# Graph attention with layer norm on one core: gathering rows of x itself instead of rows of a node table

## What is computed

```python
messages = x[col]                               # col = dst
gate = messages @ W_gate.T + b_gate             # one number an edge
h = messages @ W_lin.T + b_lin
seg_max = segment_max(gate, row)                # row = src
e = exp(gate - seg_max[row]); denom = segment_sum(e, row) + 1e-16
pooled = segment_sum(e / denom[row] * h, row)
x = layernorm(x + pooled @ W_out.T + b_out)
```

## Time and profile before

| | us |
|---|---|
| three runs: median (lowest to highest) | 2847.6 (2842.83 to 2848.6) |
| span of the profiled execution, first to last instruction | 2844.9 |
| DVE busy | 1676.2 |
| POOL busy | 1748.5 |
| PE busy | 1008.8 |
| ACT busy | 174.1 |

### The profile page before, as it was taken

One profiled execution on the slowest core, in us unless ns is written; L12 is line 12 of the kernel. 1 busy time (PEld: TensorE's weight loads), 2 busy tenths in 40 slices (PEclk: granted clock), 3 DMA queues, 4 the chain that ended last, 5 costly groups with the idle time before them and its releaser, 6 DMA issues.

```text
span 2844.9 us, 25631 instructions
## 1 busy us (share of the span) xinstructions
PE 1008.8 (35%) x5080; PEld 835.6 (29%) x5080; DVE 1676.2 (59%) x5604; ACT 174.1 (6%) x664; POOL 1748.5 (61%) x1792
## 2 busy tenths in 40 slices
PE   3012112225233342433334243342433424333377
PEld 3011111224232232422323233232333323233255
DVE  9969998346455464645546455464655646455454
ACT  0421110000000000000000000000000000000025
POOL 0411002777777777777777777777777777777621
PEclk9999996565566665566656556565655656566566
DMA  3020001222222222222222222222222222223924
GB/s 115 3 92 0 0 0 29 54 54 54 55 53 55 53 55 54 54 55 53 55 53 54 54 54 54 54 53 55 53 55 54 55 53 54 54 54 67 41 50 122
DMA packets 91745, 148.65 MB, mean 52 GB/s; under 512 B 30393, under 2 KB 61970, under 8 KB 91588
## 3 DMA queue, kind: packets, MB, share of 16 engines
q0 software_dynamic: 56224, 117.06, 20.8%
q1 hardware_dynamic: 34767, 31.04, 3.5%
q10 hardware_dynamic: 722, 0.20, 0.0%
HBM read 134.35 MB, written 13.83 MB: 52 GB/s over the span
## 4 chain that ended last, share of the span: by engine, by line
POOL 43%; issue 23%; DVE 17%; PE 7%; DVEq 2%; another core or an unknown queue 2%; ACT 2%; DMA 2%; ACTq 1%; POOLq 0%
POOL arena L375 42%; DVE spread L916 3%; DVE nodes_sb L922 2%; PE bank L590 2%; PE bank L634 2%; DMA arena<-node_table,gather_at 1%; DVE rows_b L751 1%; DVE rows_a L750 1%; DVE rows_a L751 1%; POOL gate_prod L362 1%; DVE rows_b L750 1%; ACT gate_junk L430 1%; DVEq L952 1%; DVE turn_b L751 1%
## 5 line engine op out<-in xcount | busy, mean ns | idle before, releaser
L375 POOL DMA_INDIRECT arena<-node_table,gather_at x1757 | 1675.1, 953 | 790.6 <-issue 530.3
L590 PE MATMUL bank<-arena,spread 128*128 128x129 f32 x3520 | 736.9, 379 | 334.5 <-DVE nodes_sb L922 220.6
L590 PEld LDWEIGHTS bank<-arena,spread 128*128 128x128 f32 x3520 | 642.8, 276 | 424.5 <-DVE nodes_sb L922 291.4
L916 DVE TENSOR_SCALAR spread<-iota_row,place_t,weights 128x128 f32<-128x128 f32 x1760 | 599.0, 357 | 184.7 <-PE bank L590 83.0
L922 DVE SCALAR_TENSOR_TENSOR nodes_sb<-nodes_sb,weights,bank 128x129 f32 x1760 | 605.6, 344 | 55.2 <-PE bank L590 10.5
L894 DVE TENSOR_TENSOR_SCAN run_max<-pen,bank 40x128 f32<-40x128 f32 (+1 forms) x45 | 18.5, 411 | 756.8 <-PE bank L572 756.8
L572 PE MATMUL bank<-ident,arena 128*40 128x128 f32 (+1 forms) x45 | 17.3, 384 | 703.0 <-DMA arena<-node_table,gather_at 703.0
L572 PEld LDWEIGHTS bank<-ident,arena 128*40 128x40 f32 (+1 forms) x45 | 5.4, 119 | 711.0 <-issue 711.0
L552 PE MATMUL bank<-ident,dst_f 40*128 40x40 f32 x44 | 13.1, 297 | 235.7 <-DVEq L725 234.2
L542 PE MATMUL bank<-ident,rows_a 128*128 128x128 f32 x112 | 28.1, 429 | 180.0 <-DVE rows_a L776 144.7
L446 ACT ACTIVATE gather_at<-bank 128x40 int32<-128x40 f32 x44 | 8.9, 203 | 1258.6 <-PE bank L557 1229.2
(11 more groups left out here) (161 smaller groups left out, 1066.0 us busy)
## 6 DMA issues: line engine op xcount, KB each, us to landing
arena<-node_table,gather_at POOLq DMA_INDIRECT x1757, 20.6
node_table<-nodes_sb SPq DMA_DIRECT2D x1, 6347.7 KB
nodes_sb<-in_x SPq DMA_DIRECT2D x1, 6250.0 KB
rows_a<-in_x SPq DMA_DIRECT2D x13, 448.0 KB, 4.1
out<-rows_b SPq DMA_DIRECT2D x13, 448.0 KB, 3.3
k<-sorted_keys SPq DMA_DIRECT2D x132, 20.0 KB
turn_a<-in_src SPq DMA_DIRECT2D x1, 828.0 KB
turn_b<-in_dst SPq DMA_DIRECT2D x1, 828.0 KB
```

Source lines behind the costliest of these rows:

```text
L375: pool.indirect_dma_start(out=gathered_rows[par][:, t, :], out_offset=None, in_=table[:, :], in_offset=bass.IndirectOffsetOnAxis(ap=gather ...
L590: last = pe.matmul(tile_ps(slot), lhsT=spread[:, slot, :], rhs=gathered_rows[par][:, b * BATCH + u, 0:WIDTH], start=True, stop=True)
L916: return dve.tensor_scalar(spread[:, slot, :], iota_row[:, :], place_t[par][:, t:t + 1], weights[par][:, 0, t:t + 1], ALU.is_equal, ALU.mult)
```

## The change

The node table, its load, its ten products, its 101 activations and its store are gone. The gather reads rows of 512 bytes (128 floats) from `x`. The column of ones is set once, in both buffers, by POOL after the histogram (`hist_ready`). DVE computes gates when a chunk's rows are there: `find_gates` multiplies the rows by `wg`, which it has put into PSUM once (`wg_ps`), and sums 129 terms a row, the last of which is the bias that ACT has placed. DVE instead of PE now waits for the gathered rows; PE waits for `gates_found`. `sums` has memory of its own, and POOL zeroes it right at the start.

```diff
-        nodes_sb = sb("nodes_sb", [P, 13000])
+        sums = sb("sums", [P, BLOCKS * WIDTH]).ap()
+        gate_terms = arena[:, 14000:14000 + T * WIDTH].rearrange("p (t f) -> p t f", f=WIDTH)
+        gates = sb("gates", [P, T])
...
-            sp.dma_start(node_rows[:, :, 0:FEAT], x.rearrange("(p n) f -> p n f", n=NODE_COLS)).then_inc(x_loaded, 16)
-
-            sp.wait_ge(gates_ready, 1)
-            sp.wait_ge(ones_ready, 1)
-            sp.dma_start(table.rearrange("(p n) f -> p n f", n=NODE_COLS), node_rows).then_inc(table_stored, 16)
             sp.wait_ge(zero_ready, 1)
             sp.dma_start(skeys[0:1].rearrange("(a n) -> a n", a=1), zero_key[:, :]).then_inc(keys_stored, 16)
+            sp.wait_ge(iotas_ready, 1)
...
             pool.drain().then_inc(iotas_ready, 1)
 
-            pool.wait_ge(x_loaded, 16)
-            pool.wait_ge(weights_loaded, 16 * 6)
-            pool.memset(node_rows[:, :, FEAT:FEAT + 1], 1.0).then_inc(ones_ready, 1)
-            for c in range(NODE_COLS // GATE_COLS):
-                if c > 0:
-                    pool.wait_ge(prod_used, c)
-                pool.tensor_tensor(gate_prod[0:NODE_ROWS], node_rows[:, c * GATE_COLS:(c + 1) * GATE_COLS, 0:FEAT],
-                                   wg[0:NODE_ROWS].unsqueeze(1).to_broadcast([NODE_ROWS, GATE_COLS, FEAT]),
-                                   ALU.mult).then_inc(prod_ready, 1)
-
-            pool.wait_ge(table_stored, 16)
             pool.memset(sums, 0.0).then_inc(sums_blank, 1)
 
             pool.wait_ge(hist_ready, 1)
+            for par in range(2):
+                pool.memset(gathered_rows[par][:, :, FEAT:WIDTH], 1.0)
+            pool.drain().then_inc(ones_ready, 1)
...
-                    pool.indirect_dma_start(out=gathered_rows[par][:, t, :], out_offset=None, in_=table[:, :],
+                    pool.indirect_dma_start(out=gathered_rows[par][:, t, 0:FEAT], out_offset=None, in_=x[:, :],
...
             act.wait_ge(weights_loaded, 16 * 6)
-            for c in range(NODE_COLS // GATE_COLS):
-                act.wait_ge(prod_ready, c + 1)
-                for n in range(GATE_COLS):
...
-            act.activation(node_rows[:, :, FEAT + 1], gate_sum[0:NODE_ROWS, :], ACT.Identity,
-                           bias=bg[0:NODE_ROWS, 0:1]).then_inc(gates_ready, 1)
+            act.wait_ge(hist_ready, 1)
+            act.activation(gate_terms[:, :, FEAT], bg[:, 0:1].to_broadcast([P, T]), ACT.Copy).then_inc(bias_placed, 1)
...
             def turn_softmax(i, par, n=T):
 
+                pe.wait_ge(gates_found, i + 1)
                 pe.nop(nofuse=True)
-                pe.transpose(gate_rows[0:n], gathered_rows[par][:, 0:n, FEAT + 1], ident[:, :]).then_inc(gates_turned, 1)
+                pe.transpose(gate_rows[0:n], gates[:, 0:n], ident[:, :]).then_inc(gates_turned, 1)
...
-                    pe.wait_ge(rows_gathered[par], 16 * T * j + 16 * T)
                     turn_softmax(i, par)
...
+            dve.tensor_copy(wg_ps, wg[:, :])
...
+            def find_gates(par, at, n):
+                dve.tensor_tensor(gate_terms[:, at:at + n, 0:FEAT], gathered_rows[par][:, at:at + n, 0:FEAT],
+                                  wg_ps.unsqueeze(1).to_broadcast([P, n, FEAT]), ALU.mult)
+                dve.drain()
+                dve.tensor_reduce(gates[:, at:at + n], gate_terms[:, at:at + n, :], AX.X, ALU.add)
+                dve.drain().then_inc(gates_found, 1)
...
                     prepare(i + 1, j + par, 1 - par)
+                    dve.wait_ge(rows_gathered[par], 16 * T * j + 16 * T)
+                    find_gates(par, 0, T)
                     softmax(i, par)
                     add_tiles(i, i + 1, par, range(NB))
...
+            dve.wait_ge(rows_gathered[1], 16 * T * (CHUNKS // 2 - 1) + 16 * EARLY)
+            find_gates(1, 0, EARLY)
             softmax(CHUNKS - 1, 1, EARLY)
             add_tiles(CHUNKS - 1, CHUNKS, 1, range(EARLY // BATCH))
+            dve.wait_ge(late_gathered, 16 * (TILES - (CHUNKS - 1) * T - EARLY))
+            find_gates(1, EARLY, T - EARLY)
             softmax(CHUNKS, 1)
```

More of the change, by code:

```diff
@@ L79, in check_shapes @@
 def check_shapes():
-    assert P * MAIN_COLS + REST_ROWS * REST_COLS == EDGES and NODE_ROWS * NODE_COLS == NODES
+    assert P * MAIN_COLS + REST_ROWS * REST_COLS == EDGES
     assert EARLY % BATCH == 0 and CHUNKS % 4 == 0 and (CHUNKS - 1) * T + EARLY < TILES <= CHUNKS * T and (CHUNKS + 1) * T * P < KEYS + TAIL_ROWS * P
@@ L97, in sem @@
             return ctx.enter_context(nc.semaphore(name))
-        table = nc.dram_tensor("node_table", (NODES, ROW), F32).ap()
         skeys = nc.dram_tensor("sorted_keys", (1 + KEYS + TAIL_ROWS * P,), I32).ap()
@@ L114, in graph_attention @@
         part2_i = arena[:, 23 * EDGE_COLS // 2:23 * EDGE_COLS // 2 + EDGE_COLS].bitcast(I32)
[L115 to L118, removed]
+        gathered_rows = [arena[:, k * T * WIDTH:(k + 1) * T * WIDTH].rearrange("p (t f) -> p t f", f=WIDTH) for k in range(2)]
+        gate_terms = arena[:, 14000:14000 + T * WIDTH].rearrange("p (t f) -> p t f", f=WIDTH)
+        gates = sb("gates", [P, T])
         wg = sb("wg", [P, FEAT])
@@ L344, in _ @@
             sp.wait_ge(stored[1], 16 * (GROUPS // 2 + 1))
-            sp.wait_ge(table_stored, 16)
         @block.gpsimd
@@ L425, in _ @@
             act.wait_ge(weights_loaded, 16 * 6)
-            for c in range(NODE_COLS // GATE_COLS):
-                act.wait_ge(prod_ready, c + 1)
-                for n in range(GATE_COLS):
-                    at = c * GATE_COLS + n
-                    last = act.activation(gate_junk[0:NODE_ROWS], gate_prod[0:NODE_ROWS, n, :], ACT.Copy,
-                                          accum_out=gate_sum[0:NODE_ROWS, at:at + 1])
-                    act.drain()
-                act.drain().then_inc(prod_used, 1)
-            act.activation(node_rows[:, :, FEAT + 1], gate_sum[0:NODE_ROWS, :], ACT.Identity,
-                           bias=bg[0:NODE_ROWS, 0:1]).then_inc(gates_ready, 1)
+            act.wait_ge(hist_ready, 1)
+            act.activation(gate_terms[:, :, FEAT], bg[:, 0:1].to_broadcast([P, T]), ACT.Copy).then_inc(bias_placed, 1)
             for k, back, g, _ in turning:
@@ L886, in _ @@
             dve.wait_ge(sums_blank, 1)
+            dve.wait_ge(bias_placed, 1)
+            dve.wait_ge(weights_loaded, 16 * 6)
+            dve.tensor_copy(wg_ps, wg[:, :])
             dve.drain().then_inc(sums_added, 2 * BATCH)
+            def find_gates(par, at, n):
[4 more added lines that the diff above has]
+                dve.drain().then_inc(gates_found, 1)
             def softmax(i, par, n=T):
@@ L974, in _ @@
             prepare(CHUNKS - 1, CHUNKS // 2 - 1, 1)
+            dve.wait_ge(rows_gathered[0], 16 * T * (CHUNKS // 2))
+            find_gates(0, 0, T)
             softmax(CHUNKS - 2, 0)
             add_tiles(CHUNKS - 2, CHUNKS - 1, 0, range(NB))
+            dve.wait_ge(rows_gathered[1], 16 * T * (CHUNKS // 2 - 1) + 16 * EARLY)
+            find_gates(1, 0, EARLY)
             softmax(CHUNKS - 1, 1, EARLY)
             add_tiles(CHUNKS - 1, CHUNKS, 1, range(EARLY // BATCH))
+            dve.wait_ge(late_gathered, 16 * (TILES - (CHUNKS - 1) * T - EARLY))
+            find_gates(1, EARLY, T - EARLY)
             softmax(CHUNKS, 1)
```

19 lines of the change are left out of this document (6 added, 13 removed).

## The result

| | median us (lowest to highest) | ratio to the kernel before, 95% interval |
|---|---|---|
| kernel before | 2845.2 (2840.2 to 2848.6) | |
| changed kernel | 2820.8 (2820.4 to 2833.3) | 0.9921 [0.9899, 0.9944] |

The profiled execution has a span of 2819.4 us, 25.5 less than before, where the forecast had 15.0.

What follows compares the result with a forecast made beforehand. No engine bounds it throughout: DVE's serial sort, then POOL's gather issue, then an exposed end. Terms -17.1 - 25.7 + 7.1 + 0.5 + 0 + 20.2 = -15.0 on span 2844.9 gave 2829.9, so median 2832.6 us, range 2813 to 2855.

Steps and rivals of the forecast that it cites:

- The sort, -42.8: Sort before the gathers: removing the node table ends seven held DVE instructions (-17.1 us) and DVE's wait for ACT (-25.7 us).
- The memset, +7.1: Kernel start: the moved memset of sums holds DVE's cast until it ends, +7.1 us; bounds from 0 to held.
- Behind the histogram, +0.5: After the histogram: two small memsets and the iota may hold a small DVE operation, +0.5 us, at most 1.
- The loop, 0: Gather loop: 11.3 us of new DVE gate work a chunk hides in 13.8 us of slack, so 0 us.
- Rival A: Loop: gates outlast the slack, a chunk takes half the excess longer; about 2899 us; chance 9%.
- rival B: Loop: DVE's long operations keep POOL from issuing gathers; +198 us, 3031 us; chance 6%.
- the slack: Loop: 13.8 us between indices being ready and POOL needing them; 2.5 us left on average after the gates.
- The end, +20.2: Behind the last chunks gates are exposed: +11.3 for chunk 42, +5.3 early part, +3.6 late part.
- the forecast's own bounds for it: End: 13.8 us if the first delay, PE's late start on chunk 42, is covered too; 24.6 if there is no delay.
- C: Loop: unseen waits eat the cover, +13 us and 1 to 2 at the end; 2847 us, no change; chance 10%.
- D: Loop: the shorter row makes each gather 0.1 us cheaper, a chunk 46.8 us; about 2682 us; chance 5%.

Runs made afterwards that it cites:

- row 6400: Kernel before, all padding edges pointing to row 6400 in the middle of the table instead of row 0: 2844.7 us, ratio 0.9997.
- the sum twice: Changed kernel, each chunk's tensor_reduce in find_gates done twice: 2916.8 us, ratio 1.0249.
- spread rows: Padding edges read rows all over the table instead of row 0: 2819.1 us on the kernel before, 2808.4 us on the changed kernel.
- one sum in ten: Kernel before with all ten POOL products, but ACT sums only one node of ten: 2834.4 us, ratio 0.9963.
- ten tiles more: Changed kernel, ten tiles of each chunk summed once more in find_gates: 2827.5 us, ratio 0.9944.

## Why the prediction was right, point by point

- **The sort, -42.8**: right in sum, and the trace bears both parts out, -17.1 of held exchanges and -25.7 of waiting for ACT. But the parts are not separate prices. Shorter sums alone turned seven holds into ten, and moved the memset onto an operation that it holds. Without the products, 5.53 us of the 25.71 of waiting were left, so the products had made most of that wait too.
- **The memset, +7.1**: right, 6.9 in the trace, 6.8 in the run that moves it. No row of before decided between 0 and 7.1; the choice by the nearest row was a guess that came true.
- **Behind the histogram, +0.5**: nothing of it can be seen.
- **The loop, 0**: right. Product 5.49 and sum 5.53 us, as worked out from rows of other operations. Rival A's rule (half of the excess) and rival B's mechanism are real, and both were near: a second sum costs 96 us, the weights in SBUF 174. That a two-input operation holds a gather was read from the wrong row, as said above, and shown only by the run with the weights in SBUF. The step that was off is the slack, 13.8 us from the end of ACT's copies to POOL's next gather. POOL can start only 0.8 us after those copies end (1017.39, to 1018.21), and the shorter border of each pair decides. 11.3 us used up all but 1.2 to 1.5 of it, not all but 2.5.
- **The end, +20.2**: the term that was mis-sized; measured +8.4, plus 3.2 in the stretch before it, since the last chunk's first gather waited for its indices (53.38 us behind that of chunk 42, 50.23 before), 11.6 in all. That is below the forecast's own bounds for it, 13.8 to 24.6 (the second is 24.1 by its own terms, 11.3 + 5.3 + 7.5). The failed step is "some delay of PE on leaving its loop, which outlived the wait. I take it to come again behind the gates". There was no such delay: the rows came late, by reads of one row. The gates then lay in part under lateness that was there anyway. The scan of chunk 42 came 7.3 us later against the last gather, not 11.3, and the early scan another 1.0, not 5.3; beside it lies a stall of PE that took 10.6 us up to 2670 in the kernel before and 6.6 up to 2640 here. The late scan lost 3.5 (forecast 3.6) and stands 36.0 us behind the last gather, not 44. The stall, in the kernel before and then in the changed one:

```profile
2670.45 2.74 PE L590 MATMUL bank<-arena,spread 128*128 128x129 f32 x12 [10.62 <-issue]
```
```profile
2639.77 2.74 PE L565 MATMUL bank<-arena,spread 128*128 128x129 f32 x12 [6.56 <-issue]
```

  With the lateness removed from both kernels the end costs 25.5 us, near the forecast's own bound for no delay.
- **The output stage, not in the forecast**: 107.3 us from its first product on, 110.3 before. It goes with TensorE's granted clock in that stage, here for the kernel before, with row 6400, and with the sum twice (stretch, length, clock, DMA share, GB/s):

```profile
2734.65:2844.90 110.25, 0.69 0.39 108
```
```profile
2735.30:2848.60 113.30, 0.67 0.38 105
```
```profile
2813.70:2915.80 102.10, 0.78 0.43 117
```

  The levels are 0.5 (1.2 GHz) and 1.0 (2.4 GHz), and these are means between them. In all thirteen kernels the stage takes 110 to 113 us at 0.67 to 0.70, 105 to 107 at 0.72 to 0.76 (0.72 in the changed kernel, 0.73 and 0.72 with spread rows), and 102 at 0.78. So some 3 of the 25.5 us of span are no work of this change. They aren't the late reads of one row either: with one sum in ten, and with ten tiles more, these reads are there and the stage takes 105 us. Why the clock was what it was is not shown.
- **Rivals**: nothing in the runs speaks for C or D. POOL never waits between the chunks of the loop, and gathers of 512 and 520 bytes take the same 0.94 us.

So the forecast of the span was 10.5 us off (15.0, measured 25.5): 8.6 in the end (20.2, measured 11.6, of it 3 by the clock), 1.2 in the loop, where chunks are some 0.03 us shorter, and 0.7 at the start. The old kernel had a fault at its end that hid 14 us of the new work (25.5 - 11.6). Where that fault is mended first, the same change is worth 10.7 us instead of 24.

## What to carry to other kernels

A precomputed table that keeps other engines busy during a serial stage can cost more than many times its arithmetic done later, if that is done beside a stage set by something else (here 42.8 us against 485 us of new DVE work); but measure the cover there by the tightest of the waits that go round, and find the part behind the last overlap, where all of it shows. Place a long POOL memset beside DVE operations with two SBUF inputs, and a long DVE operation beside POOL with one input in PSUM. Let padding indices point to different rows: an idle time "for a DMA" that ends later than issue and usual landing explain should send one to the DMA share of that stretch before an engine is blamed.

## What the runs showed of the hardware

- **Many reads of one row are slow.** A gather of 128 times the same row moves 40 GB/s at a DMA share of 0.9, against 53 at 0.24 for different rows: 128 x 520 bytes at 40 GB/s are 1.66 us a gather, some 13 ns a read (an estimate from these rates), and more than POOL's 1.25 us between issues, so the queue runs late, by some 48 x 0.4 = 20 us at the end. In the changed kernel with 512 bytes it is 128 x 512 at 39 GB/s = 1.68 us. Whether it goes by reads or by bytes these runs can't tell: the rows differ by 1.6%, the rate of one kernel from stretch to stretch by more (37 to 44 GB/s).
- Beside it engines stand still at code that they run for the first time, waiting for nothing that the profile shows: PE for 10.6 us in the kernel before and 12.3 with row 6400, DVE for 4.99 in the changed one. With spread rows PE's is gone and DVE's is 2.40. But PE's stall is also missing, or no longer than 1.6 us, in two kernels that do read one row, those with the weights in SBUF and with ten tiles more. What makes these stalls is not shown.
- **A POOL memset holds a single-input DVE operation to its end** (9.17 us for 0.18; 8.49 for 0.76) and leaves two-input ones alone (0.55, 0.69). The Trainium skill has it so, by ports that single-input operations may take and a writer shares, while two inputs contend only with a GpSimd instruction that reads (SBUF — State Buffer, Who interferes with whom); the traces agree.
- **A DVE operation with two SBUF inputs holds a gather that begins during it** for all that is left of it: 5.09 us or more instead of 0.94, once in each of 43 chunks; with one input in PSUM no gather takes over 1.23 us, and the mean stays 0.953.
